# Per-step node numbers turned to rows by TensorE instead of through DRAM, and a reset mask stored once, in the opening of a two-layer graph network on one Trainium2 core

## The reference

```
edge_index = jnp.stack([src, dst])
x = x + _L0_gnn_ref(_layernorm(x, axis=-1), edge_index, L0_gnn_W, ...)
...
h = (x @ W.T).reshape(N, H, F)                       # rows gathered per edge later
alpha = einsum(h[src], a_src) + einsum(h[dst], a_dst)
alpha = jnp.where(alpha >= 0, alpha, 0.2 * alpha)
seg_max = jax.ops.segment_max(alpha, dst, num_segments=N)
exp_a = jnp.exp(alpha - seg_max[dst])
seg_sum = jax.ops.segment_sum(exp_a, dst, num_segments=N)
msgs = h_src * (exp_a / seg_sum[dst])
agg = jax.ops.segment_sum(msgs, dst, num_segments=N)
```

## Time and profile before

| | |
|---|---|
| median of 3 runs | 1969.44 us |
| the profiled execution's own time | 1970.59 us |
| its span | 1968.9 us |
| mean granted TensorE clock | 0.818 |
| busy: PE, VectorE, ScalarE, GpSimd | 70%, 75%, 53%, 53% |
| opening: first instruction to the start of `edges_first` | 0 to 75.37 us |
| gathers of `edges_first` | 76.1 to 616 us |

### The profile page before, as it was taken

How to read it: one execution, slowest core, us unless ns; L and a number is a source line. 1 busy time by engine, 2 the same in 40 slices (tenths; PEclk the granted TensorE clock), 3 DMA queues, 4 the chain that set the end, 5 groups by cost and what they waited for, 6 DMA issues and landing times. The chain is left out here.

```text
span 1968.9 us, 29222 instructions
## 1 busy us (share of the span) xinstructions
PE 1369.7 (70%) x7038; PEld 951.1 (48%) x7038; DVE 1469.7 (75%) x3724; ACT 1038.9 (53%) x3518; POOL 1052.8 (53%) x1131
## 2 busy tenths in 40 slices
PE   5346666566566579998957778787877888663286
PEld 4224444344344557775534555555555554452165
DVE  5468889888888923547778999999999997676043
ACT  2435555555654442332514888878888888231032
POOL 2377777777773000003167777777777776100554
PEclk9767778778777679998977988989989888775598
DMA  5744444444442055002477766766767673215564
GB/s 121 198 131 130 141 130 127 141 129 128 141 127 60 1 172 205 1 1 86 160 232 221 204 199 198 202 189 194 202 202 199 199 205 115 84 57 110 188 192 126
DMA packets 141111, 287.85 MB, mean 146 GB/s; under 512 B 25507, under 2 KB 66977, under 8 KB 140821
## 3 DMA queue, kind: packets, MB, share of 16 engines
q0 software_dynamic: 58192, 175.85, 31.1%
q1 hardware_dynamic: 82758, 110.13, 19.2%
HBM read 241.17 MB, written 48.86 MB: 147 GB/s over the span
## 5 line engine op out<-in xcount | busy, mean ns | idle before, releaser
L775 POOL DMA_INDIRECT e_rows<-h_rows,src_col x416 | 413.6, 994 | 127.0 <-issue 122.1
L1245 POOL DMA_INDIRECT e_rows<-kv_rows,src_col x320 | 308.6, 964 | 99.2 <-issue 58.3
L1019 PE MATMUL e_sum<-e_rows,e_of_dst 128*128 128x264 f32 x832 | 293.9, 495 | 85.8 <-DVE e_rows L865 71.7
L1486 ACT ACTIVATE e_rows<-e_rows 128x64 f32<-128x64 f32 x1152 | 289.0, 336 | 0.3
L1565 PE MATMUL e_query<-q,e_to_dst 128*128 x1248 | 215.6, 309 | 93.4 <-DVE e_rows L1313 70.6
L1019 PEld LDWEIGHTS e_sum<-e_rows,e_of_dst 128*128 128x128 f32 x832 | 175.9, 239 | 128.6 <-DVE e_rows L865 79.2
L1606 PE MATMUL e_sum<-e_rows,e_of_dst 128*128 128x260 f32 x640 | 205.1, 447 | 1.5 <-DVE acc L1401 0.7
L1565 PEld LDWEIGHTS e_query<-q,e_to_dst 128*128 128x128 bf16 x1248 | 124.6, 104 | 149.6 <-issue 108.2
L946 ACT ACTIVATE e_rows<-e_rows 128x32 f32<-128x32 f32 x832 | 181.0, 305 | 0.1
L1401 DVE TENSOR_TENSOR acc<-acc,e_sum 128x260 f32 x299 | 125.9, 421 | 55.5 <-PE e_sum L1606 23.8
L1606 PEld LDWEIGHTS e_sum<-e_rows,e_of_dst 128*128 128x128 f32 x640 | 122.1, 214 | 29.1 <-DVE acc L1401 10.8
(11 more groups left out here) (420 smaller groups left out, 2932.4 us busy)
## 6 DMA issues: line engine op xcount, KB each, us to landing
sorted_rows<-zeros SPq DMA_DIRECT2D x1, 14560.0 KB
rows<-sorted_rows SPq DMA_DIRECT2D x56, 260.0 KB, 2.9
e_rel<-step_rel SPq DMA_DIRECT2D x26, 512.0 KB, 4.1
e_to_dst<-step_rel SPq DMA_DIRECT2D x52, 256.0 KB, 3.9
e_rows<-h_rows,src_col POOLq DMA_INDIRECT x416, 2.8
e_to_typ<-step_typ SPq DMA_DIRECT2D x52, 128.0 KB
e_rows<-kv_rows,src_col POOLq DMA_INDIRECT x320, 3.8
kv_rows<-kv SPq DMA_DIRECT2D x5, 768.0 KB, 3.5
```

The source lines that it names most:

```text
L775: pool.indirect_dma_start(out=g[t // BATCH % R][:, t % BATCH, :], out_offset=None, in_=k.h_rows[:, :], in_offset=bass.IndirectOffsetOnAxis ...
L1019: pe.matmul(psm[t % NB], of_dst[q][:, s % GROUP, :], g[m % R][:, s, :], start=True, stop=True).then_inc(summed, 1)
L1245: pool.indirect_dma_start(out=rows_at(t, 1)[:, 0, :], out_offset=None, in_=k.kv_rows[:, :], in_offset=bass.IndirectOffsetOnAxis(ap=k.src_c ...
L1486: ins = act.activation(x, x, ACT.Copy, scale=row[:, plo + h:plo + h + 1])
```

## The change

Five edits. The stores and reloads of the ends and windows through DRAM go, and with them SyncE's wait for the mark `ends` and the wait for the 12 stores. `ends_f` is written eight times side by side, so that a matmul with the identity as moving operand puts it on 8 partitions; TensorE does this in `rows_over_steps`, 12 matmuls of 104 columns ahead of `turn(20)`, and the windows go the same way. VectorE copies the last ends and the windows out of PSUM in `joins_of_steps` (the cast `win_i` goes, `win_row` is cast from PSUM). The mask is stored once (`step_cut`), by one DMA ahead of `store_rows(2)`, and the loads of both edge stages repeat each row 8 or 4 times. SyncE's last wait is for 5 stores instead of 24 and 2 loads.

```diff
-    k.step_cut8 = dram("step_cut8", [STEPS, H0, P + 4], F32)
-    k.step_cut4 = dram("step_cut4", [STEPS, H1, P + 4], F32)
-    k.step_ends = dram("step_ends", [2, STEPS], F32)
-    k.step_win = dram("step_win", [1, STEPS], I32)
+    k.step_cut = dram("step_cut", [STEPS, P + 4], F32)
...
-                c.link(v.tensor_copy(win_i[:, :], win_f[:, :]))
...
-                c.inc(v.tensor_copy(ends_f[:, 0, :], rows_f[:, :, 0, 0]))
-                c.inc(v.tensor_copy(ends_f[:, 1, :], rows_f[:, :, 0, P - 1]))
-                marks["ends"] = c.count
+                eight = [SP, SC, 8]
+                c.inc(v.tensor_copy(ends_f[:, 0, :, :], rows_f[:, :, 0, 0].unsqueeze(2).to_broadcast(eight)))
+                c.inc(v.tensor_copy(ends_f[:, 1, :, :], rows_f[:, :, 0, P - 1].unsqueeze(2).to_broadcast(eight)))
...
             def joins_of_steps():
-                v.wait_ge(reread, 32)
                 c.link(v.memset(k.joined[:, :, :], 1.0))
-                c.link(v.tensor_tensor(k.joined[:, 0, 1:STEPS], ends_r[:, 0, 1:STEPS], ends_r[:, 1, 0:STEPS - 1],
+                v.wait_ge(pe_done, 4)
+                first, last = ps_a[0:8, 0:STEPS], ps_b[0:8, 0:STEPS]
+                c.inc(v.tensor_copy(ends_r[:, :], last))
+                c.inc(v.tensor_copy(k.win_row[:, 0:STEPS], wins))
+                c.wait()
+                c.link(v.tensor_tensor(k.joined[:, 0, 1:STEPS], first[:, 1:STEPS], ends_r[:, 0:STEPS - 1],
                                        ALU.not_equal))
...
+            def rows_over_steps():
+                pe.wait_ge(k.dve_steps, marks["columns"])
+                for sc in range(SC):
+                    at, one = slice(sc * SP, (sc + 1) * SP), k.ident[0:SP, 0:SP]
+                    pe.matmul(ps_a[0:8, at], ends_f[:, 0, sc, :], one, start=True, stop=True)
+                    pe.matmul(ps_b[0:8, at], ends_f[:, 1, sc, :], one, start=True, stop=True)
+                    mm = pe.matmul(wins[:, at], win_f[:, sc:sc + 1], one, start=True, stop=True)
+                mm.then_inc(pe_done, 1)
+
             for w in range(WIN + 1):
                 if w == 2 * UNR:
                     columns()
+                if w == 4 * UNR:
+                    rows_over_steps()
...
-            sp.wait_ge(k.dve_steps, marks["ends"])
-            for j in range(2):
-                for c4 in range(SC):
-                    sp.dma_start(k.step_ends[j:j + 1, c4 * SP:(c4 + 1) * SP].rearrange("o p -> p o"),
-                                 ends_f[:, j, c4:c4 + 1]).then_inc(stored, 16)
-            for c4 in range(SC):
-                sp.dma_start(k.step_win[0:1, c4 * SP:(c4 + 1) * SP].rearrange("o p -> p o"),
-                             win_i[:, c4:c4 + 1]).then_inc(stored, 16)
             store_rows(0)
             store_rows(1)
-            sp.wait_ge(stored, 12 * 16)
-            sp.dma_start(ends_r[:, :, :].rearrange("p j s -> p (j s)"),
-                         k.step_ends[:, :].rearrange("j s -> (j s)").partition_broadcast(8)
-                         ).then_inc(reread, 16)
-            sp.dma_start(k.win_row[:, 0:STEPS], k.step_win[:, :]).then_inc(reread, 16)
             sp.wait_ge(k.dve_steps, marks["stores"])
...
-            store_cuts(H0, k.step_cut8)
+            sp.dma_start(k.step_cut[:, :].rearrange("(c p) e -> p c e", p=SP), cut[:, :, :]).then_inc(stored, 16)
             store_rows(2)
-            store_cuts(H1, k.step_cut4)
             store_rows(3)
             store_rows(4)
-            sp.wait_ge(stored, 24 * 16)
-            sp.wait_ge(reread, 32)
+            sp.wait_ge(stored, 5 * 16)
...
-            sp.dma_start(cut[m % R][:, :], k.step_cut8[m * BATCH:(m + 1) * BATCH, :, :].rearrange("s h e -> (s h) e")
-                         ).then_inc(cut_in[m % R], 16)
+            steps = k.step_cut[m * BATCH:(m + 1) * BATCH, :]
+            sp.dma_start(cut[m % R][:, :],
+                         steps.unsqueeze(1).to_broadcast([BATCH, H, P + 4])).then_inc(cut_in[m % R], 16)
```

More of the change, by code:

```diff
@@ L244, in prepare_and_project @@
         win_f = sb("win_f", [SP, SC])
-        win_i = sb("win_i", [SP, SC], I32)
         win_x = sb("win_x", [SP, SC])
@@ L252, in prepare_and_project @@
         cut = sb("cut", [SP, SC, P + 4])
-        ends_f = sb("ends_f", [SP, 2, SC])
-        ends_r = sb("ends_r", [8, 2, STEPS])
+        ends_f = sb("ends_f", [SP, 2, SC, 8])
+        ends_r = sb("ends_r", [8, STEPS])
         single = sb("single", [8, STEPS])
@@ L275, in prepare_and_project @@
         ps_w = ps("ps0_w", [P, 2, D])
+        wins = ps_w.rearrange("p c f -> p (c f)")[0:1, 0:STEPS]
         ps_v = ps("ps0_a", [P, BANK])[:, 0:DC * 2 * H0].rearrange("p (c j) -> p c j", c=DC)
@@ L283, in prepare_and_project @@
         stored = sem("prep_stored")
-        reread = sem("ends_reread")
         x_in = [sem(f"x_in{r}") for r in range(WROUNDS)]
@@ L389, in columns_of_steps @@
                 c.inc(v.tensor_copy(k.src_col[:, :], ps_b[:, 0:STEPS]))
+                marks["columns"] = c.count
             def joins_of_steps():
-                v.wait_ge(reread, 32)
                 c.link(v.memset(k.joined[:, :, :], 1.0))
-                c.link(v.tensor_tensor(k.joined[:, 0, 1:STEPS], ends_r[:, 0, 1:STEPS], ends_r[:, 1, 0:STEPS - 1],
+                v.wait_ge(pe_done, 4)
[4 more added lines that the diff above has]
+                c.link(v.tensor_tensor(k.joined[:, 0, 1:STEPS], first[:, 1:STEPS], ends_r[:, 0:STEPS - 1],
                                        ALU.not_equal))
-                c.link(v.tensor_tensor(single[:, :], ends_r[:, 0, :], ends_r[:, 1, :], ALU.not_equal))
+                c.link(v.tensor_tensor(single[:, :], first, ends_r[:, :], ALU.not_equal))
                 c.inc(v.tensor_tensor(k.joined[:, 1, 0:STEPS], k.joined[:, 0, 0:STEPS], single[:, :], ALU.max))
@@ L587, in store_rows @@
                                  h[:, first % XN:(first % XN) + hi - lo, 0:R0]).then_inc(h_kept[r % 2], 16)
-            def store_cuts(H, dst):
-                for c4 in range(SC):
-                    sp.dma_start(dst[c4 * SP:(c4 + 1) * SP, :, :],
-                                 cut[:, c4, :].unsqueeze(1).to_broadcast([SP, H, P + 4])).then_inc(stored, 16)
             for j, name in enumerate(("dst", "src", "edge_type_64")):
@@ L1213, in load_cut @@
             b = m % 2
-            sp.dma_start(cut[b][:, :], k.step_cut4[m * LONG:(m + 1) * LONG, :, :].rearrange("s h e -> (s h) e")
-                         ).then_inc(cut_in[b], 16)
+            steps = k.step_cut[m * LONG:(m + 1) * LONG, :]
+            sp.dma_start(cut[b][:, :],
+                         steps.unsqueeze(1).to_broadcast([LONG, H, P + 4])).then_inc(cut_in[b], 16)
         for h in two:
```

## The result

The changed kernel took 1957.42 us, the median of 5 runs (1952.35 to 1959.92). Beside them the kernel before took 1969.09 (5 runs, 1962.95 to 1969.87). The ratio is 0.9936 [0.9915, 0.9958]: 11.7 us less, where 5.7 were forecast and 1961.5 was the low end of the range. The prediction was wrong in its size. The profiled execution took 1952.35 us, with a span of 1950.6 and a mean granted clock of 0.824; it is the shortest of the five, 5.1 under their median, so the difference of the two spans (18.3 us) is more than the kernels differ by. In all that follows, ratios, and the means of e17 and e18, leave out runs that are over 1.5% above the fastest of the same kernel.

What follows compares the result with a forecast made beforehand. It took the opening's node projection, then stages paced by GpSimd's gathers, as bounding the time. Terms 5.6 + 0.7 + 1.5 - 1.8 - 0.6 + 0.3 = 5.7 us took 1969.44 to 1963.7; range 1961.5 to 1966.9.

Steps and rivals of the forecast that it cites:

- `take(10)`, with the gather's loss in it: ScalarE's `take(10)` no longer waits for round 0's stores: 5.6 us saved, less 0.6 for the edge-tile gather beside a store.
- `take(10)` to the root of round 3: Without TensorE's slow clock after the first hole, this stretch of the opening falls from 3.3 to 2.6 us: 0.7 saved.
- second hole: ScalarE's wait before `take(20)` for round 2's stores goes, bringing `turn(24)` closer behind `turn(23)`: 1.5 us saved.
- 12 new matmuls: TensorE's added matmuls ahead of `turn(20)` cost 2.1 us less 0.27 of idle: a loss of 1.8 (1.3 to 4.0).
- last landing: The last store at the opening's end lands sooner because the queue is emptier: 0.3 us saved (0 to 1.0).
- opening: Stretch before `edges_first`, which would start at 69.7 instead of 75.37 us: 5.7 saved.
- behind the opening: All stages after the opening keep their length, so the opening's gain is carried to the end at full value.
- reading of SyncE's queue: Round 0's stores were issued late behind 12 small stores and landed in 10.7 to 11.1 us, a backlog of tiny writes.
- the cast: Sign: VectorE's cast of gathered edge tiles (L370) starts at 34 to 35 us; beyond 36 would be wrong.
- rival in which the first stores stay slow: First `h_rows` stores still land in 10.9 us, moving the hole to `take(15)`: gain 1.3, 1968.1 us; chance 0.10.
- slower rival: Last gather beside round 0's first store lands 10.9 us after 31.1, losing 7.9 instead of 0.6: 1971.0 us; chance 0.06.
- rival for that part: Later stages lose the gain through clock and waits: half lost gives 1966.6 us, all 1969.4; chance 0.12.

Runs made afterwards that it cites:

- e17: Changed kernel with VectorE's statistics of round 2 earlier, labels and mask later, eight new matmuls ahead of window 10; second timing, on a slower chip: ratio 0.9938 to before.
- e18: The kernel of e17 with two dead VectorE memsets at the end of the opening, same chip: ratio 0.9999 to before.
- e4: Kernel before with only round 0's stores issued ahead of the small stores, on a slower chip: ratio 0.998.
- e2: Kernel before with only the turning of the ends by TensorE, mask still stored 8 and 4 times, on a slower chip: ratio 0.9963.
- e3: Kernel before with only the mask stored once and spread by the loads, small stores kept, on a slower chip: ratio 1.0043.
- e9: Changed kernel with twelve dead stores of 4-byte elements between rounds 0 and 1, on a slower chip: ratio 0.9974 to before.
- e10: Same kernel as e3, mask alone stored once, run again on the second slower chip: ratio 0.9989 to before.
- e15: Changed kernel with four dead VectorE memsets at the end of the opening: 1964 is not its time but 1969.48 us, ratio 0.9996 to before.
- e1: Changed kernel again without edit, against the kernel before, on a slower chip: ratio 0.9973.

## Why the prediction was wrong

Point by point, in us earlier than before:

| step | forecast | measured |
|---|---|---|
| `take(10)`, with the gather's loss in it | 5.6 - 0.6 = 5.0 | 51.72 - 46.62 = 5.1 |
| `take(10)` to the root of round 3 | 3.3 to 2.6: 0.7 | 3.32 to 2.61: 0.7 |
| second hole | 1.5 | root of round 4 to the last copy, without the matmuls: 1.5 |
| 12 new matmuls | -1.8 | 2.1 less the idle time: root of round 4 was 5.95 ahead, `turn(20)` 4.05: -1.9 |
| last landing | 0.3 | 4.15 to 68.34 - 65.64 = 2.70: 1.45 |
| opening | 5.7 | 7.0 (6.4 in the means of three traces) |
| behind the opening | 0 | 3.2 to 3.9 (with 6.4: 3.8 to 4.5) |
| all | 5.7 | 10.2 to 10.9 |

**Right**: the mechanism, and four of the five terms of the opening within 0.1 us, against the very trace that they were read from. (The remaining 0.15 of the opening lies between the roots of rounds 3 and 4, 6.31 us before and 6.17 now.) The reading of SyncE's queue held: the landings were 2.2 to 3.6 us once the small stores were gone, the cast came at 34.65, the twelve matmuls cost what was priced from a window's two. The rival in which the first stores stay slow has fallen: in e4 round 0's stores landed in 2.2 and 3.7 us ahead of the small ones and round 1's in up to 10.0 behind them. The slower rival has fallen too: with a store beside the gather the cast came 0.57 us later, not 7.9.

**The step that failed** is in the first paragraph: "Everything behind it is separated by ends of blocks, so I carry the opening's gain to the end at full value." The opening gave 6.4 to 7.0, the whole 10.2 to 10.9 with a standard error of 1.0, so 3 to 4 us lie behind the opening, where the prediction put nothing. Its rival for that part knew only a loss. The delayed kernels show that the time follows the start, at 1.27 to 1 over all runs and at about 1.2 to 1 on one chip, neither clearly over 1. By the line 7.0 us of start are worth 8.9, and 1.3 to 2.0 stay open; at one to one 3.2 to 3.9 do. The table of stages puts the surplus into several stages and no single one, with the choice of executions in all of them; only the 2.5 us between the last gather and the second edge stage go with the single mask at every start. The cause of the surplus stays open. No wait in the first edge stage answers for it: GpSimd's waits there for TensorE, the row that answers to the earlier trace rows, are as small as before.

```profile
POOL e_rows L767 <- PE e_sum L1011: 5.2, 17, 0.3
```

One lead is the clock: over the 131 runs on the faster chips, compared within each kernel, an execution whose mean granted clock is 0.001 higher is 0.70 us shorter, and the means are 0.8235 for the changed kernel and 0.8219 for the one before. That would be 1.1 us. It is a correlation, and no run sets the clock.

**The mis-sized term** inside the opening is the last landing, 0.3 where it was 1.45. The prediction knew that the engines were busy for 1.02 of the time, and that the queue would be emptier; it took 0.3 of a range of 0 to 1.0 and its upper end was short as well. Of the mask's 12 copies 11 went, some 2.4 MB or 10 us of a queue that had been busy for all of 62 to 71 us, and a queue that no longer is full lands a 264 KB store in 2.2 us. The two halves of the change bear it out: 4.45 us at the end with the copies (e2), 2.78 without them (e3).

**The range** was also built on too little jitter. The bounds of the prediction's own terms add up to 2.1 to 7.5, not to the "2.7 to 8" that it states. It took three runs within 0.8 us for the spread. The kernel before goes from 1962.0 to 1979.2 over 73 runs, with a standard deviation of 3.6, so a median of five runs moves by about 2 us from one set to the next. Even so 1958.3, the median of 19, lies under its low end: the miss is more than the spread of the runs.

## What to carry to other kernels

A store of 4-byte elements is paid for by what is queued behind it: look at the landing times of the big stores, not at the small ones' own issue, and at who waits for them, since e4 only moved the wait. The holes of an opening can be priced from the timelines, but the opening itself moves by 1 to 1.6 us between executions of one kernel, so trace the kernel before more than once. Carry the gain to the end as a range that is open on both sides: here the whole moved by 3 to 4 us more than the opening. A small delay in a place that changes nothing else shows how the time follows the start; three delayed kernels with 10 to 12 runs each could not tell a factor of 1.27 from 1 with certainty. And before a difference of 0.3% is explained, run the kernel before against itself.

## What the runs showed of the hardware

- Twelve stores of 104 elements of 4 bytes (5 KB together) kept the 16 DMA engines at 0.98 of their time in 42 to 46 us while 53 GB/s moved (e9), and in e3 stores of 264 and 396 KB behind them landed in 9.6 to 10.0 us, against 2.2 to 3.6 without them.
- In the same place of the program a pause of TensorE of 4.01 us was followed by 0.57 of the clock (4 us), one of 2.83 by 1.00 (e9), one of 2.84 by 0.66 (e10). In e15 it was 0.50 up to 48, behind a pause of 4.28, and its round took 9.06 us instead of 7.72.
- 104 columns of f32 with a stationary operand of 8 or of 1 columns take 0.18 us at the full clock.
- Chips differ: 2150 to 2180 us on two of them and 1958 to 1970 on the others for the same kernels. Most of it lies in the stages that gather rows: 661 instead of 539 us in the first and 761 instead of 685 in the second (e1 beside the first trace).
